# Per-head score products over 32 partitions into four banks, in a kernel of three attentions and an expert layer

## The reference

```python
# compressed: 225 keys and values, each a two-layer net over a 4x4 patch of keys
attn_cmp = softmax(einsum('bhnd,bhmd->bhnm', q_c, kch) * SCALE)   # 1024 x 225 per head
out_cmp = einsum('bhnm,bhmd->bhnd', attn_cmp, vch)
# selected: the 16 patches that the compressed attention weighs most
imp = attn_cmp.sum(axis=1).mean(axis=1)
_, idx = top_k(imp, 16)
attn_slc = softmax(einsum('bhnd,bhmd->bhnm', q_s, ksh) * SCALE)   # 1024 x 256 per head
out_slc = einsum('bhnm,bhmd->bhnd', attn_slc, vsh)
# window: 7x7 windows with a bias table
out = g0 * proj(out_cmp) + g1 * proj(out_slc) + g2 * out_win
x = x + out
t = t + weighted sum of two of eight experts(layernorm(t))
```

## Time and profile before

| | us |
|---|---|
| median of 3 runs | 748.17 |
| lowest and highest run | 747.45, 748.37 |
| the profiled execution, its own time | 749.96 |
| its span in the trace | 748.2 |
| TensorE busy | 662.0 (88%) |
| VectorE, ScalarE busy | 439.9 (59%), 443.2 (59%) |
| POOL busy | 233.8 (31%) |
| mean granted TensorE clock | 0.952 |

### The profile page before, as it was taken

One profiled execution on the slowest core, in us unless ns is written; L12 is line 12 of the kernel. 1 busy time (PEld: TensorE's weight loads), 2 busy tenths in 40 slices (PEclk: granted clock), 3 DMA queues, 4 the chain that ended last, 5 costly groups with the idle time before them and its releaser, 6 DMA issues.

```text
span 748.2 us, 16869 instructions
## 1 busy us (share of the span) xinstructions
PE 662.0 (88%) x5318; PEld 496.9 (66%) x5318; DVE 439.9 (59%) x1429; ACT 443.2 (59%) x1287; POOL 233.8 (31%) x341
## 2 busy tenths in 40 slices
PE   2997899999899999989999999877899998989992
PEld 1694467666557766555776656554468897989981
DVE  4206847553986754488676548777646653455443
ACT  1307844664883366487336648633767896878961
POOL 3200014200202473110247310042605477644551
PEclk9999999999999999989999998985899999999995
DMA  7301000000000010000001090001301334363215
GB/s 293 126 0 30 1 1 6 2 0 29 29 2 2 4 35 25 29 1 1 3 4 37 24 264 18 1 5 48 77 8 38 132 86 103 84 200 93 73 47 179
DMA packets 36353, 40.03 MB, mean 54 GB/s; under 512 B 12176, under 2 KB 27936, under 8 KB 35980
## 3 DMA queue, kind: packets, MB, share of 16 engines
q1 hardware_dynamic: 30412, 27.47, 12.8%
q0 software_dynamic: 4704, 9.40, 3.8%
q10 hardware_dynamic: 1152, 2.10, 0.8%
HBM read 25.64 MB, written 15.17 MB: 55 GB/s over the span
## 4 chain that ended last, share of the span: by engine, by line
PE 62%; DVE 16%; ACT 9%; issue 5%; DMA 3%; SPq 2%; POOL 2%; DVEq 1%; ACTq 0%; POOLq 0%
PE ps L1713 8%; PE ps L1788 8%; PE ps L1830 6%; PE ps L1773 6%; PE ps L2173 6%; PE ps L1718 5%; PE ps L2191 5%; PE ps L1860 3%; ACT r_P L927 3%; DVE nmx L1241 2%; PE ps L1890 2%; PE ps L1933 2%; PE ps L1875 2%; PE ps L1902 1%; DVE r_P L1251 1%
## 5 line engine op out<-in xcount | busy, mean ns | idle before, releaser
L927 ACT ACTIVATE r_P<-ps,nmx 128x225 f32<-128x225 f32 (+1 forms) x192 | 86.0, 468 | 62.6 <-DVE nmx L1241 62.6
L1241 DVE TENSOR_REDUCE nmx<-ps 128x4 f32<-128x900 f32 (+1 forms) x64 | 73.7, 1156 | 24.7 <-PE ps L1830 24.1
L778 POOL DMA_INDIRECT xs_d<-pay,pos x64 | 62.4, 974 | 35.9 <-DVE nmx L1241 20.8
L800 POOL DMA_INDIRECT z_d<-xhatT,xrow_room x54 | 52.7, 977 | 61.9 <-DVE xhatT L1632 55.2
L702 POOL TENSOR_TENSOR rstd<-vpe,minus_half 128x8 f32<-128x8 f32 x8 | 13.6, 1701 | 187.0 <-DVE vpe L1178 187.0
L1713 PE MATMUL ps<-ident,r_P 128*128 128x128 f32 (+1 forms) x384 | 54.6, 284 | 13.0 <-DVE R L1263 7.7
L1713 PEld LDWEIGHTS ps<-ident,r_P 128*128 128x128 f32 (+1 forms) x384 | 45.7, 152 | 26.7 <-issue 9.8
L1620 DVE TENSOR_TENSOR hv<-ps,x_sb 128x128 f32<-128x128 f32 x78 | 22.7, 291 | 67.8 <-PE ps L2191 51.4
L752 POOL TENSOR_TENSOR r_gh<-r_gh,nmw 113x392 f32<-113x392 f32 (+1 forms) x20 | 15.6, 781 | 140.5 <-DVE nmw L1280 140.3
L1788 PEld LDWEIGHTS ps<-r_vc,w_sb 128*128 128x128 f32 x256 | 46.1, 188 | 19.4 <-issue 15.9
L1788 PE MATMUL ps<-r_vc,w_sb 128*128 128x225 f32 x256 | 58.8, 375 | 0.0
(11 more groups left out here) (242 smaller groups left out, 1461.6 us busy)
## 6 DMA issues: line engine op xcount, KB each, us to landing
xrow_room<-xs_d SPq DMA_DIRECT2D x54, 65.0 KB, 2.0
x_sb<-x SPq DMA_DIRECT2D x4, 512.0 KB, 3.5
w_sb<-w1k SPq DMA_DIRECT2D x1, 2048.0 KB, 7.6
w_sb<-w1v SPq DMA_DIRECT2D x1, 2048.0 KB, 12.1
w_sb<-fw SPq DMA_DIRECT2D x1, 2048.0 KB, 9.7
w_sb<-fw SPq DMA_DIRECT2D x4, 512.0 KB, 10.0
r_vw<-z_d SPq DMA_DIRECT2D x8, 256.0 KB, 4.0
out<-x_tok ACTq DMA_DIRECT2D x8, 256.0 KB, 2.2
```

The lines of the kernel that those rows point to most:

```text
L778: gp.indirect_dma_start(xs_d, bass.IndirectOffsetOnAxis(pos[:, NT * k + t:NT * k + t + 1], 0), pay[:, k, t, :], None).then_inc(scattered, 16)
L800: gp.indirect_dma_start(z_d, bass.IndirectOffsetOnAxis(xrow(n)[:, C + 1:C + 2].bitcast(U32), 0), yrow(n), None).then_inc(y_out[n % XRING], 16)
L927: last = sc.activation(Pb[t % NRING][:, h, 0:m], bank(name)[:, (h % 2) * m:(h % 2) * m + m], ACT.Exp, bias=nmx[:, t % NRING, h:h + 1], acc ...
L1241: ve.tensor_reduce(nmx[:, t % NRING, :].rearrange("p (a h) -> p a h", a=2), v.rearrange("p a (h m) -> p a h m", h=2), AX.X, ALU.max, negat ...
```

## The change

A tile's scores are now four products, one per head, over that head's 32 partitions, into banks 0, 1, 2 and 3; every tile uses all four. The keys stand once in `kbd`, without masks: one operation each writes them on ScalarE (compressed) and on VectorE (selected), the memset of `kbd` on POOL and a column of biases are gone. TensorE claims all four banks before the first product, with a no-op behind the claims. `maxima` is two operations of two heads; ScalarE's first two exponentials wait for the first, the others for the second, and each exponential frees its bank. In both stages the scores move behind the extras of their step. The copy of mk moves before the last window group on ScalarE, since bank 3 is needed earlier.

```diff
         def scores(s, t, b):
-        for k in range(2):
-            put(2 * (t % 2) + k, f"S{s}{t}{'ab'[k]}@{b}")
+        for i in range(HEADS):
+            put(i, f"S{s}{t}{i}@{b}")
...
-    kbd = sb("kbd", [128, 2, 256])
+    kbd = sb("kbd", [128, 256])
...
-            gp.memset(kbd[:, :, :], 0.0).then_inc(zeroed, 1)
...
             def key_blocks(h):
-                for k, (mask, bias) in enumerate((("even", "b2ke"), ("odd", "b2ko"))):
-                    last = sc.activation(kbd[:, k, 0:NB], bank(name)[:, 0:NB], ACT.Identity, bias=col(bias), scale=col(mask))
+                copy_out(f"k2@{h}", kbd[:, 0:NB], bank(f"k2@{h}")[:, 0:NB], bias=col("b2k"))
...
             def exps(b, s, t, m):
-                act.wait_ge(max_ready, b * 2 * NT + (NT if s == "s" else 0) + t + 1)
                 for h in range(HEADS):
+                    if h % 2 == 0:
+                        act.wait_ge(max_ready, 2 * (b * 2 * NT + (NT if s == "s" else 0) + t) + h // 2 + 1)
...
             def window_stage(b):
+                    if g == NGRP + 1 and h < B:
+                        copy_out(f"mk@{h}", hk[:, :, :].rearrange("p a m -> p (a m)"), bank(f"mk@{h}")[:, 0:2 * NB])
...
             def maxima(b, s, t, m):
-                ve.tensor_reduce(nmx[:, t % NRING, :].rearrange("p (a h) -> p a h", a=2),
-                                 v.rearrange("p a (h m) -> p a h m", h=2), AX.X, ALU.max, negate=True)\
-                  .then_inc(max_ready, 1)
+                for i in range(0, HEADS, 2):
+                    ve.tensor_reduce(nmx[:, t % NRING, i:i + 2], two_banks(f"S{s}{t}{i}@{b}")[:, :, 0:m],
+                                     AX.X, ALU.max, negate=True).then_inc(max_ready, 1)
...
             def selected_keys(b):
-                for h in range(HEADS):
-                    p0, p1 = HD * h, HD * h + HD
-                    last = ve.scalar_tensor_tensor(
-                        out=kbd[p0:p1, h % 2, :].rearrange("p (k i) -> p k i", i=NPOS), in0=kflip[p0:p1, :, 1, :],
-                        scalar=col("m1", p0, p1), in1=khalf[p0:p1, :, :], op0=ALU.mult, op1=ALU.add)
+                ve.scalar_tensor_tensor(
+                    out=kbd[:, :].rearrange("p (k i) -> p k i", i=NPOS), in0=kflip[:, :, 1, :],
+                    scalar=col("m1"), in1=khalf[:, :, :], op0=ALU.mult, op1=ALU.add).then_inc(kbd_sel_ready, 1)
...
             def scores(b, s, t, m):
-                for k in range(2):
-                    claim(name)
-                    p0 = 64 * k
-                    mm(bank(name)[:, 0:2 * m], q[p0:p0 + 64, 128 * t:128 * t + 128],
-                       kbd[p0:p0 + 64, :, 0:m], start=True, stop=True).then_inc(full_sem(name), 1)
+                for h in range(HEADS):
+                    claim(f"S{s}{t}{h}@{b}")
+                pe.nop(nofuse=True)
+                for h in range(HEADS):
+                    name, p0 = f"S{s}{t}{h}@{b}", HD * h
+                    mm(bank(name)[:, 0:m], q[p0:p0 + HD, 128 * t:128 * t + 128], kbd[p0:p0 + HD, 0:m],
+                       start=True, stop=True).then_inc(full_sem(name), 1)
```

43 lines of the change are left out of this document (16 added, 27 removed).

## The result

The changed kernel takes 773.41 us (median of 4 runs, 771.51 to 778.08) against 748.27 (747.45 to 750.17). The ratio is 1.0342, with a 95% interval of 1.029 to 1.0393. The forecast was 756 us: the sign was right, the size was not. The time lies inside the range, but the loss is three times the 7.9 us that were summed.

The account below looks back on a forecast made before the run. TensorE bounds selected tiles of images 0 to 2; compressed tiles mix several waits. Terms 1.9 + 2.6 + 2.6 + 1.3 − 3.0 + 2.5 = +7.9 us, added to the 748.17 median: 756 us, range 745 to 774.

Parts of the forecast that it names:

- serial-strips rival: Scores on TensorE: four row strips may run no faster than two pairs; +20, 776 us, chance 0.10.
- the products: Selected scores on TensorE: four products take 0.64 us instead of 1.06, saving 0.42 a tile.
- the loop in the selected stage: Claiming all four banks makes scores wait for the last exponential; selected tile 3.62 us instead of 3.77, TensorE's remaining saving idle.
- the wake-up: Between the last exponential and the scores: a released claim with a no-op behind it, 0.11 us.
- faster rival: Compressed tiles stay bound by VectorE, so only key write, half maximum and shorter scores count; 738 us, chance 0.18.
- cancelling one: Losses of some 8 to 11 us and gains of some 3, in small terms, cancel; 748 us, chance 0.10.
- the compressed tiles: Compressed stage: exponentials, copy, extra, scores, maximum stand in a row; images 0 to 3 lose 1.9, 2.6, 2.6, 1.3 us.
- The key write and the half maximum: End of window stage: one key write saves 1.46 us an image; a two-head maximum starts ScalarE 0.54 us earlier.
- the order: Compressed stage: TensorE does extras before the next scores, and the third extra's bank waits for ScalarE's exponentials; this costs time.
- image 3: Selected stage without value layer, partly at 1.2 GHz: cycles 3.62 to 4.05 us, net +2.5 us, between +1.1 and +4.2.

Follow-up runs that it names:

- the kernel with all fillers: Changed kernel plus idle identity products on TensorE ahead of some score claims, in compressed image 0 and the selected stages of all images; 777.2 us, ratio 1.0365.
- the order alone: Kernel before with only the scores moved behind the extras and the value layer, two pairs of banks and four key writes kept; 767.6 us, ratio 1.0225.
- the two with fillers: Changed kernel with idle identity products ahead of some score claims: in many places, 777.2 us; cut back, with none in image 3, 777.0 us.

## Why the prediction was right in sign and wrong in size

The range of 745 to 774 holds the 773.4 only because its upper end was drawn to take in half of the serial-strips rival; the forecast's own bounds were 749 to 764. That the time fell inside is luck, for that rival did not come true.

**Right: the products.** The serial-strips rival, which had the nearest time (776), is out: four products over four row strips take 0.64 us, as taken from the gate's hidden layer. The Trainium skill, "TensorE: Matmul & The Clock Gate", section "Measured speedup vs the span model", gives 3.07 times for four row tiles. Here eight records of 256 columns one after another would be 1.75 × 256/225 = 1.99 us, an estimate from the earlier trace rows, so the 0.64 is 3.1 times; the trace agrees. The prediction's "some 0.1 us earlier" by that figure does not come out: 1.99/3.07, again an estimate, is 0.65 us, the time that the sum had taken anyway.

**Right: the loop in the selected stage.** The cycle is made of the terms that were written down, and the gain of 0.42 us on TensorE became idle time. The term that was off is the wake-up: 0.22 instead of 0.11 us, from a single case with one claim to four claims and a no-op. Seven cycles are 0.8 us longer by it, and images 0 to 2 together 2.3 of the 2.7 that were missed there; tile 2 of image 0, at the low clock, is the rest. The Trainium skill has the reason for the loop in "TensorEngine Tiling (Array Packing)", section "Gotcha 1: PSUM Pressure": row tiles that run together need banks of their own. No run here puts two strips into one bank; the kernel gives each of the four its own, and so each tile takes all the banks that two tiles had shared. The faster rival (738) and the cancelling one (748) are out as well: the compressed tiles did not keep their spacing, and they lost more than everything else gave.

**Right: the key write and the half maximum.** 1.47 and 0.54 us an image. In images 0 and 1 the window stage gave back 0.8 and 0.7 instead of 1.9, since the transposes of the last compressed tiles ran at the low clock; with the clock at full, as in the kernel with all fillers, it is 2.0.

**Wrong: the compressed tiles, +10.6 us summed, +18.3 measured.** This is the largest part of what was missed, 7.7 of the 14.3 us by which the profiled execution lies above the forecast's column. The step that failed is the one that took every duration of TensorE in that chain from rows of before, at full clock, and so put the low clock at nothing there without a reason. The mechanism, the order, is right, and the order alone brings it about. In image 1, where the clock stayed nearest to its old value, the tiles stood at 3.5, 12.3, 18.8, 24.5, 30.6 and 36.2 us after tile 0 (tiles 1 and 3 to 7), forecast 3.4, 12.2, 18.5, 24.1, 29.8 and 35.1 (the terms written for tile 7 add up to 35.0). In images 0, 2 and 3 the clock fell further. The serial chain itself leaves TensorE idle ahead of the claims and of the extras; that this is the cause is shown for image 0, by the fillers, and only read from the rows for the others. I had priced the low clock only where before showed it, in image 3's selected stage.

Image 0 gives the size: 31.3 us at 0.95 and 32.9 at 0.72, of a forecast 30.15; so 1.6 of its 2.7 us are the clock, and the rest is the wake-up and what else the chain holds. For the others four kernels can be compared that have the same compressed program from image 1 on: the change, the one with four key writes and the two with fillers. In image 3 tiles 4 and 5 came 4.01 and 6.38 us behind the tile before at a clock of 0.50 and 0.53, and 3.54 and 5.38 with four key writes at 1.00 and 0.91. The shortest time of each tile among the four gives 35.6, 36.6 and 31.6 us for images 1 to 3; the forecast was 35.1, 36.2 and 31.2, the change took 36.2, 37.7 and 33.5. By this estimate the chain's own terms were some 0.5 us short an image, and 0.6, 1.1 and 1.9 us came with the falls of the clock, with image 0 some 5 of the 7.7. In one execution as a whole only 1.4 of it is seen: with four key writes image 3 took 32.1 us at 0.89, where the change took 33.5 at 0.80. The Trainium skill has this in "TensorE: Matmul & The Clock Gate", section "A second HAM failure mode: psum-queue depth-cycling": a kernel that cycles through PSUM banks can idle between its groups so often that the clock swings. The trace agrees, with 0.72 against 0.94, and that rule would have told me to price these stages at both clocks.

**Wrong in size: image 3.** +7.1 between its selected tiles 0 and 7 lies just above what was given (+3.9 to +7.0). Three terms were short. Two cycles at the low clock are 4.3 us instead of the 4.05 taken (0.5 to 0.6 more than at full clock, where 0.43 was counted), the other cycles 3.72 instead of 3.62 by the wake-up, and ahead of tile 7 ScalarE has a copy and the weights of two experts:

```profile
561.25 0.60 ACT L842 ACTIVATE xtT<-ps 128x512 f32<-128x512 f32 x1 [1.10 <-PE ps L1701]
...
562.17 1.28 ACT L1085 ACTIVATE wx_room<-w_sb 128x518 f32 x2 [0.32 <-ACT xtT L842]
...
563.37 0.46 ACT L921 ACTIVATE r_P<-ps,nmx 128x256 f32<-128x256 f32 x1
```

So tile 7 comes 5.63 us behind tile 6, 1.9 more than a cycle, where 0.6 was counted: the copy of 0.60 had been left out and the weights counted at half.

**Open.** The +2.5 us after the last tile can't be read: with the same code there, this stretch took 203.5 to 208.2 us in the kernels of this study. For images 1 to 3 the share of the clock is an estimate from executions whose clock fell in different places, since tiles lean on those before them; no run held the clock up there alone.

## What to carry to other kernels

Faster products that need more banks can cost the second set of banks, and then a tile is a sum of latencies; write that cycle down before counting the gain, and look for a claim that is half as wide. An instruction that waits at the head of a queue holds up all that stands behind it: with the loop closed the scores were better behind the extras, with it open better ahead of them in the one stage and behind in the other. When a change adds idle time to TensorE, price its steps at both clock levels wherever the new chain has idle time, not only where the old trace shows the low one.

## What the runs showed of the hardware

The granted clock of one and the same stage, with the same program, was 0.89 in one kernel and 0.83 in two others, 36.2 against 39.4 and 39.5 us. That is 3 us on one stage from nothing in it, more than most edits here are worth. Two executions with the same instructions up to that point took 32.5 us at 0.88 and 31.3 at 0.95 for image 0's compressed stage, on two chips, so it moves without any edit; and the longest execution of the changed kernel, 778.1 us, is the one with the lowest mean clock, 0.913. Four claims and a no-op cost 0.17 us more on the chain than one claim.
